# Four-layer GNN on one core: the attributes' copy issued behind the step gathers, first keys inside the histogram, equality matrices from bf16 rank numbers, half of the zero fills issued last by ScalarE

## The chip, the cores and the metric

The kernel runs on one core of a Trainium2 chip as one program. Its time is the device time in microseconds of one execution, given as the median of several. Engine names in rows: PE is TensorE (PEld its weight loads), DVE is VectorE, ACT is ScalarE, POOL is GpSimd, SP is SyncE, which here only issues DMAs. Sixteen DMA engines serve all queues of the core.

## The reference, cut to what matters

The input is a graph of 3125 nodes with 128 features, 50,000 edges sorted by destination (`src`, `dst`), and 64 attributes for each edge. Four layers follow one another, each on relu(layernorm(x)), each added to x:

```
L0 GCN:   h = (h * rsqrt(deg_out)) @ W; agg = segment_sum(h[src], dst) * rsqrt(deg_in) + b
          out = relu(layernorm(agg) * gamma + beta) + h
L1 attn:  q[dst] . (k[src] + e) / 4, e = edge_attr @ We; softmax over each dst; sum of (v[src] + e)
          8 heads of 16; skip, layernorm, gelu FFN, layernorm
L2 GAT:   two GAT layers (3 heads, then 1), softmax over each dst, elu between
L3 SAGE:  two mean aggregations with linear maps and batch norm
```

Out-degrees, in-degrees and, for the attention layers, which edges of a block share a destination, are computed on the device from `src` and `dst`.

## The kernel before, in words

Edges are padded to 50,176 (`EP`) and seen as 392 blocks of 128 (`CH`), and as 98 groups of 4 blocks (`NG`, `GC`). Each engine has its own program, written out by hand; semaphores order them, and each engine and each DMA queue goes through its list in order. The change touches the first part of the program, in three stages.

**Preparation.** SP lists `src` and `dst` in HBM (`esrc`, `edst`), then fills `eattr`, the attributes with each block of 128 rows turned round (`fill`, L690): that is a copy of 49,920 rows of 256 bytes. VectorE computes for 1172 "steps" (`STEPS`, in 10 chunks of 128, `NC`) which edge block and which quadruple of nodes each belongs to, and hands the indices to GpSimd, which gathers 128 rows of `esrc` and of `edst` for each chunk (L978, L981: 20 gathers, `step_edges`). Meanwhile VectorE builds one-hots of `src` for a histogram of out-degrees in 25 turns (`hot`, `HTURNS`; TensorE multiplies them, L1447), and then waits for all 20 gathers, turns those of the first two chunks (`SOON`) into keys (`key_steps`), and enters the loop. TensorE transposes the keys (`keys_of`), ScalarE copies them out (`keys_copied`).

**The adjacency loop**, 147 batches (`NB`) of 8 steps. For a batch VectorE writes two one-hots (`hot_steps`: 1024 and 800 elements a partition), TensorE multiplies them into counts (L1488), ScalarE copies these into the adjacency matrix of the chunk (L1080). VectorE is at most three batches ahead of TensorE. From batch 17 on TensorE also runs the GCN product of the chunk before (`spmm`, L1474). When a chunk is complete, SP stores its 3200 KB (`store_adj`, L740); two chunks' room is alternated. From batch 20 on (`SAME0`) VectorE makes in addition one equality matrix for each group, about three in four batches (`same`, L2136):

```
tt(same_b[:, r, :, :], dst_row[:, r, :, ::-1],
   bc(dst_i[:, g * GC:(g + 1) * GC]..., [P, GC, P]), ALU.is_equal)
```

It compares the destination of each edge of a block with those of all 128 edges of the block. `dst_row` holds a group's 512 destinations on every partition, loaded by SP as int32 four groups ahead (`load_dst_row`, L724, `UNROLL`), and `same_b` goes to HBM (`store_same`, L731). On SP's list each group is a store, a load, sometimes a zero fill of `starts_q` (L746, 28 fills of 896 KB with groups 10, 12, ... 64) and at eight groups an adjacency store.

**The node stage** behind the loop: TensorE ends the products and sums them by node; ScalarE and VectorE copy out (`pick`), in-degrees give the index lists, then linear maps, norms, and q, k, v. GpSimd scatters rows of q into `starts_q`, which must be zero by then (`s_zero`). The attention pass reads `eattr` by groups, transposes it on TensorE, and ScalarE copies it out (`attr_sb`).

Of the kernel before, what the change touches and what calls it, by code (L numbers as in the profile page):

```python
# [13 lines left out]
P = 128  # L14
# [55 lines left out]
LATE_AT = 5  # L70
SPANS_AT = 40
# [109 lines left out]
def gnn_stack_kernel(nc, out, x, src, dst, edge_attr_64, **w):  # L181
    ctx = ExitStack()
    with ctx:
# [3 lines left out]
        def sem(name):  # L187
            return ctx.enter_context(nc.semaphore(name))
# [9 lines left out]
        breaks = hbm("breaks", [CH + 1, P + 2])  # L198
        same_hbm = hbm("same_hbm", [NG, P, GC * P], BF16)
# [18 lines left out]
        dst_i = sb("dst_i", [P, CH], I32)  # L218
# [79 lines left out]
        def place(at, parts, *dims):  # L298
# [66 lines left out]
                             "dst_row": (P, (UNROLL, GC, P), I32)}, work_at)  # L365
        iota_two, lo_t, key_t, hot_e, hot_k, dst_row = (
            work[k] for k in ("iota_two", "lo_t", "key_t", "hot_e", "hot_k", "dst_row"))
        block_i = dst_row[:, 0, :, :].rearrange("p k e -> p (k e)")[:, 0:CH]
# [21 lines left out]
                        "lo_f": (P, (CH,), BF16), "hi_f": (P, (CH,), BF16)})  # L390
        src_r, dst_r, prev_r, src_rf, dst_rf, brk_r = (prep[k] for k in ("src_r", "dst_r", "prev_r", "src_rf", "dst_rf", "brk_r"))
        part_i, lo_f, hi_f = (prep[k] for k in ("part_i", "lo_f", "hi_f"))
# [10 lines left out]
            "rank_i": (P, (3, CH), I32), "pay": (P, (5, GC), I32), "attr_k": (P, (GC, ED), F32)})  # L403
# [21 lines left out]
        s_hist = sem("s_hist")  # L425
        wp = tuple(WEIGHTED)
# [12 lines left out]
        step_edges = sem("step_edges")  # L439
# [41 lines left out]
        FILLS = 16 * 4  # L481
        ZERO_PARTS = 28
# [107 lines left out]

        def units(ch):

            return slice(ch * DG, ch * DG + (DG if ch < NC - 1 else 1))
# [55 lines left out]
        def _(sp):  # L649
# [38 lines left out]
            def fill(o, i):  # L688
# [4 lines left out]
            fill(eattr[E - tail:E - tail + P - tail, :], zrow[0:P - tail, 0:ED])  # L693
            fill(eattr[EP - P:EP, :], zrow[:, 0:ED])
            fill(eattr[FULL * P + P - tail:FULL * P + P, :].rearrange("t (s c) -> s t c", s=2),
                 edge_attr_64[FULL * P:E, :].rearrange("t (s c) -> s t c", s=2)[:, ::-1, :])
            fill(eattr[0:FULL * P, :].rearrange("(t p) c -> t p c", p=P),
                 edge_attr_64[0:FULL * P, :].rearrange("(t p) c -> t p c", p=P)[:, ::-1, :])
# [21 lines left out]
            def load_dst_row(g):  # L720
                r = g % UNROLL
                if g >= UNROLL:
                    sp.wait_ge(same_done.sem, same_done.at("gcn", g, UNROLL))
                sp.dma_start(dst_row[:, r, :, :].rearrange("p k e -> p (k e)"),  # L724
                             edst[P + g * GC * P:P + (g + 1) * GC * P].rearrange("(a n) -> a n", a=1)
# [27 lines left out]
            for g in range(UNROLL):  # L753
                load_dst_row(g)
# [1896 lines left out]
```

## Time and profile before

| | us |
|---|---|
| median of 3 runs | 2823.56 |
| lowest, highest | 2819.49, 2824.34 |
| the profiled execution | 2818.55 |
| its span in the profile | 2816.9 |

| engine | busy us | share of the span |
|---|---|---|
| TensorE | 1962.1 | 70% |
| VectorE | 1420.3 | 50% |
| GpSimd | 1385.7 | 49% |
| ScalarE | 963.1 | 34% |

These shares are averages over stages with different limits. GpSimd's time, for instance, is spent on row gathers in the attention passes, which the change does not touch; a stage has to be looked at by itself. The rows below give busy time of each engine in four stretches that together are the first 458 us, and then single instructions. A value in brackets behind a row is how long the engine was idle before it, and what ended that.

### The profile page before, as it was taken

Reading aid. Unit: us, or ns where it says so; the run is one execution under the profiler, and the core shown is the slowest. Engines: PE = TensorE matmul, PEld = TensorE weight load, DVE = VectorE, ACT = ScalarE, POOL = GpSimd, SP = SyncE. Lnnn points to the kernel's source line nnn. Section 1 sums busy time; section 2 is a strip of 40 time slices with the busy share of each in tenths; the row PEclk is TensorE's granted clock in tenths of the full one; section 3 lists DMA queues with packets and bytes.
Section 4 is the critical chain, followed back from the end, with each engine's and each line's share of the span. In section 5 each row is a group of like instructions: output and inputs, shape, how many; then the busy total and the mean of one; then the engine's idle time right before and its main releaser. Section 6 shows DMA issues by size and latency. Waiting matters only on the chain.

```text
span 2816.9 us, 33483 instructions
## 1 busy us (share of the span) xinstructions
PE 1962.1 (70%) x10859; PEld 1352.9 (48%) x10859; DVE 1420.3 (50%) x3094; ACT 963.1 (34%) x2148; POOL 1385.7 (49%) x1417
## 2 busy tenths in 40 slices
PE   3477787488888885747777777744444445499998
PEld 2344455277777774523333334433333334266666
DVE  7778774477767775634544444422222223512414
ACT  4433323333333333834444443422222222301202
POOL 6000001777777773577777771567777774300000
PEclk9899898788998895868888886875555555799999
DMA  9499960499998982157777773325555553565461
GB/s 212 134 330 385 358 225 19 137 256 259 264 267 255 262 248 58 24 141 239 235 246 236 247 242 119 90 67 130 132 132 136 132 135 89 178 203 161 138 201 33
DMA packets 518583, 517.97 MB, mean 184 GB/s; under 512 B 153344, under 2 KB 463763, under 8 KB 517227
## 3 DMA queue, kind: packets, MB, share of 16 engines
q1 hardware_dynamic: 310349, 267.63, 31.1%
q0 software_dynamic: 50528, 115.22, 16.1%
q10 hardware_dynamic: 157534, 132.98, 15.3%
q8 instruction: 89, 1.46, 0.2%
q14 instruction: 83, 0.68, 0.1%
HBM read 301.53 MB, written 227.32 MB: 188 GB/s over the span
## 4 chain that ended last, share of the span: by engine, by line
POOL 40%; PE 21%; issue 16%; DVE 11%; DMA 8%; ACT 3%; SPq 1%; POOLq 0%; ACTq 0%; DVEq 0%
POOL arena L1049 36%; PE ps L1586 10%; DMA arena<-edst 4%; DVE arena L1994 3%; PE ps L1568 2%; POOL arena L981 1%; PE ps L1857 1%; DVE same_b L2136 1%; PE ps L1474 1%; PE ps L1679 1%; DMA arena<-t_gat,src_i 1%; PE ps L1705 1%; DVE arena L2458 1%; ACT arena L1080 1%; ACT arena L1290 1%
## 5 line engine op out<-in xcount | busy, mean ns | idle before, releaser
L1080 ACT ACTIVATE arena<-ps 128x774 f32<-128x774 f32 (+8 forms) x689 | 492.8, 729 | 1142.4 <-PE ps L1679 631.6
L1049 POOL DMA_INDIRECT arena<-t_gat,src_i x784 | 741.4, 946 | 238.9 <-issue 235.3
L1679 PE MATMUL ps<-arena 128*128 128x136 f32 (+2 forms) x2352 | 688.4, 454 | 86.6 <-DVE arena L2348 81.6
L1679 PEld LDWEIGHTS ps<-arena 128*128 128x128 f32 x2352 | 460.2, 259 | 238.9 <-DVE arena L2348 115.3
L1049 POOL DMA_INDIRECT arena<-t_attn,src_i x392 | 379.9, 969 | 127.8 <-issue 112.7
L2296 DVE TENSOR_TENSOR z_b<-arena 128x12 f32<-128x12 f32 (+1 forms) x196 | 33.7, 172 | 589.3 <-DMA arena<-t_gat,src_i 581.9
L1586 PE MATMUL ps<-arena 128*128 128x384 bf16 x1850 | 304.8, 328 | 35.2 <-DVE rec L2505 32.7
L1637 PE MATMUL ps<-ident,logit 128*64 128x128 f32 (+2 forms) x147 | 47.7, 324 | 384.8 <-DVE logit L2309 324.1
L1586 PEld LDWEIGHTS ps<-arena 128*128 128x128 bf16 x1850 | 181.6, 98 | 158.2 <-issue 40.5
L2348 DVE TENSOR_TENSOR arena<-arena,ps 128x1536 f32<-128x1536 f32 (+1 forms) x196 | 229.8, 1214 | 1.6 <-ACT arena L1219 1.6
L1637 PEld LDWEIGHTS ps<-ident,logit 128*64 128x64 f32 (+2 forms) x147 | 14.1, 96 | 429.7 <-DVE logit L2309 356.1
L1008 POOL TENSOR_TENSOR arena<-arena,r_L_gnn_gamma 128x512 f32<-128x512 f32 (+1 forms) x7 | 8.1, 1155 | 402.0 <-ACT arena L1290 401.9
L1994 DVE TENSOR_TENSOR arena<-arena 128x1024 bf16<-128x1024 bf16 (+1 forms) x344 | 204.8, 648 | 0.5 <-ACT arena L1080 0.5
L1474 PE MATMUL ps<-arena 128*128 128x385 bf16 x925 | 187.4, 345 | 0.0
L2288 DVE TENSOR_TENSOR arena<-arena,ps 128x1024 f32<-128x1024 f32 x98 | 119.2, 1216 | 130.1 <-DMA arena<-t_attn,src_i 100.6
L1080 ACT ACTIVATE arena<-same_b 128x512 f32<-128x512 bf16 x294 | 167.6, 621 | 28.0 <-DMA same_b<-same_hbm 28.0
L1080 ACT ACTIVATE arena<-arena 128x512 bf16<-128x512 f32 (+4 forms) x208 | 63.9, 307 | 274.5 <-DVE arena L2601 246.5
L1488 PE MATMUL ps<-arena 128*128 128x100 bf16 x1176 | 91.8, 226 | 86.4 <-DVE arena L1994 84.5
L2601 DVE TENSOR_REDUCE arena<-ps 128x128 f32<-128x384 f32 x74 | 36.2, 551 | 220.0 <-PE ps L1586 220.0
L1488 PEld LDWEIGHTS ps<-arena 128*128 128x128 bf16 x1176 | 73.4, 107 | 125.7 <-DVE arena L1994 113.4
L1619 PE MATMUL ps<-w_e,arena 64*128 64x128 f32 x784 | 123.8, 303 | 1.2 <-DVE arena L2288 1.2
L1629 PE MATMUL ps<-arena 128*128 128x128 f32 x784 | 121.8, 302 | 0.0
(319 smaller groups left out, 2595.3 us busy)
## 6 DMA issues: line engine op xcount, KB each, us to landing
ends_gat<-arena ACTq DMA_DIRECT2D x98, 774.0 KB, 6.7
arena<-adj_hbm SPq DMA_DIRECT2D x90, 640.0 KB, 4.6
same_b<-same_hbm SPq DMA_DIRECT2D x294, 128.0 KB
adj_hbm<-arena SPq DMA_DIRECT2D x9, 3200.0 KB, 13.1
ends_attn<-arena ACTq DMA_DIRECT2D x98, 272.0 KB, 5.3
ends_gat<-arena ACTq DMA_DIRECT2D x98, 258.0 KB, 5.0
arena<-edst SPq DMA_DIRECT2D x98, 256.0 KB, 5.9
starts_q<-zrow SPq DMA_DIRECT2D x28, 896.0 KB, 7.4
```

The source lines that it names most:

```text
L1049: g.indirect_dma_start(out=row_b[:, n % RB, k, 0:row_tab[p].shape[1]], out_offset=None, in_=row_tab[p], in_offset=bass.IndirectOffsetOnAxi ...
L1080: return a.activation(o, i, ACT.Copy)
L1474: i = mm(bank(4 + n % 4)[:, 0:3 * D + 1], lhs, xs0[:, t, 0:3 * D + 1], start=t == 0, stop=t == NT - 1)
L1488: i = mm(ps[:, at:at + KEYS], hot_e[:, b % 3, e // 2, :, e % 2], hot_k[:, b % 3, e // 2, :, e % 2], start=True, stop=True)
L1586: m = mm(bank(ch % 2 * 4 + dl)[:, 0:3 * D], ring[:, u % RING, at:at + P], xs1[:, t, :, :].rearrange("p s c -> p (s c)"), start=t == 0, sto ...
L1619: i = mm(bank((1, 6)[g % 2])[:, k * D:(k + 1) * D], at_t[:, g % 2, k * P:(k + 1) * P], w_e[:, :], start=True, stop=True)
L1629: i = mm(bank((3, 7)[g % 2])[:, k * D:(k + 1) * D], same_f[:, g % RB, k, :], q_b[:, g % UNROLL, k, :], start=True, stop=True)
L1637: nc.tensor.transpose(bank(TURN_BANK[p])[0:kh, 0:P], logit[:, i % 2, 0:kh], ident[:, :])\
L1679: i = mm(o, same_f[:, g % RB, k, :], msg[:, g % 4, k * W:(k + 1) * W], start=True, stop=True)
L1994: return tt(o, bc(iota_two[:, 0:parts, :].rearrange("p (a i) s -> p a i s", a=1), [P, n, parts, 2]), bc(values.rearrange("p (a i s) -> p a ...
L2288: tt(kv, kv, bc(bank((1, 6)[g % 2]).rearrange("p (k s c) -> p k s c", k=GC, s=1), [P, GC, 2, D]), ALU.add).then_inc(kve_done.sem, 1)
L2348: tt(m[:, :, 0:heads * nc_].rearrange("p k (h c) -> p k h c", h=heads), rows_v, e, ALU.mult).then_inc(msg_done.sem, 1)
```

## The change

1. **The attributes' copy.** SP waits for a new semaphore `attr_go`, which GpSimd raises behind its 20 gathers, before it copies the attributes; everything behind it on SP's list comes after it. The copy is now straight, without the turned blocks; ScalarE turns the columns when it copies the transposed attributes out. The gathers of the first two chunks have a semaphore of their own, those of the other eight another (`late_edges`).
2. **The keys of two chunks** are computed on VectorE behind turn 12 of the histogram (`KEYS_AT`), and transposed on TensorE there.
3. **Rank numbers.** VectorE numbers the distinct destinations within each block by four scans over the breaks between destinations. They are small integers, exact in bf16. ScalarE stores them (`erank`) and loads the first four groups' rows; SP loads the rest, 128 KB each in place of 256. The comparison is of bf16 with bf16, written in pairs like the one-hots.
4. **The zero fills.** SP issues 14 of 28, with groups 8, 12, ... 60; ScalarE issues the other 14 behind its last batch. GpSimd waits for all of them ahead of the first scatter, not ahead of the node stage.

```diff
@@ SP @@
+            fill(eattr[E:E + P, :], zrow[:, 0:ED])
+            fill(eattr[E + P:EP, :], zrow[0:EP - E - P, 0:ED])
+            sp.wait_ge(attr_go, 1)
+            fill(eattr[0:E, :].rearrange("(a n) c -> a (n c)", a=1000),
+                 edge_attr_64.rearrange("(a n) c -> a (n c)", a=1000))
...
-            for g in range(UNROLL):
-                load_dst_row(g)
...
-                if g >= 10 and g % 2 == 0 and g // 2 - 5 < ZERO_PARTS:
-                    zeros(starts["attn"], ZERO_PARTS, g // 2 - 5, 256)
+                if g >= 8 and g % 4 == 0 and g // 4 - 2 < ZERO_SOON:
+                    zeros(sp, starts["attn"], ZERO_PARTS, g // 4 - 2, 256)
@@ GpSimd @@
             for ch in range(NC):
+                landed = step_edges if ch < SOON else late_edges
...
+            pool.sem_inc(attr_go, 1)
             g.memset(xs0[:, :, 3 * D:XW], 1.0).then_inc(s_ones, 1)
...
-            pool.wait_ge(s_zero, ZEROS)
...
+                if j == 0:
+                    pool.wait_ge(s_zero, ZEROS)
                 scatter("attn", j)
@@ ScalarE @@
+            act.wait_ge(rank_done, 2)
+            act.dma_start(erank.rearrange("(a t e) -> t a e", a=QA, e=P), rank_b[:, :, :]).then_inc(rank_out, 16)
...
+            act.wait_ge(rank_out, 16)
+            act.wait_ge(step_cmp, 4)
+            for g in range(UNROLL):
+                act.dma_start(dst_row[:, g, :, :].rearrange("p k e -> p (k e)"), ranks_of(g)).then_inc(dst_row_in.of(g), 16)
             act.wait_ge(s_brk, BRKS)
             for b in range(NB):
...
+            for at in range(ZERO_SOON, ZERO_PARTS):
+                zeros(act, starts["attn"], ZERO_PARTS, at, 256)
             act.wait_ge(adj_out[0], 16 * (NC // 2))
...
-                    copy(at_t[:, g % 2, :], bank(0)[0:ED, :]).then_inc(attr_sb_done.sem, 1)
+                    copy(at_t[:, g % 2, :].rearrange("c (k e) -> c k e", k=GC),
+                         bank(0)[0:ED, :].rearrange("c (k e) -> c k e", k=GC)[:, :, ::-1]).then_inc(attr_sb_done.sem, 1)
@@ TensorE @@
+            pe.wait_ge(rank_done, 1)
+            for a in range(QA):
+                i = mm(bank(3)[:, a * CQ:(a + 1) * CQ], rank_r[:, a, :], ident[0:CQ, 0:CQ], start=True, stop=True)
+            i.then_inc(rank_ps, 1)
...
             for turn in range(HTURNS):
+                if turn == KEYS_AT + 1:
+                    pe.wait_ge(step_keys, 1)
+                    keys_of(0, SOON, 0, 1)
@@ VectorE @@
-            v.tensor_copy(dst_i[:, :], ps[:, BANK:BANK + CH]).then_inc(s_small, 1)
...
+            for a in range(QA):
+                i = v.tensor_tensor_scan(rank_r[:, a, ::-1], ones[0:CQ, :], brk_r[:, a, :], 0.0, ALU.mult, ALU.add)
+            i.then_inc(rank_done, 1)
+            dve.wait_ge(rank_done, 1)
+            v.tensor_copy(rank_b[:, :, :], rank_r[:, :, :]).then_inc(rank_done, 1)
...
             for turn in range(HTURNS):
                 hot(turn)
+                if turn == KEYS_AT:
+                    dve.wait_ge(step_edges, 16 * 2 * SOON)
+                    for part_of in key_steps(0, SOON, key_math, step_keys):
+                        part_of()
...
+            dve.wait_ge(rank_ps, 1)
+            v.tensor_copy(rank_two[:, :, :], bc(bank(3)[:, 0:CH].rearrange("p (c s) -> p c s", s=1), [P, CH, 2]))
             dve.wait_ge(s_hist, HTURNS)
...
-            dve.wait_ge(step_edges, 16 * 2 * NC)
-            for part_of in key_steps(0, SOON, key_math, step_keys):
-                part_of()
...
-                tt(same_b[:, r, :, :], dst_row[:, r, :, ::-1],
-                   bc(dst_i[:, g * GC:(g + 1) * GC].rearrange("p (k c) -> p k c", c=1), [P, GC, P]), ALU.is_equal)\
+                tt(same_b[:, r, :, :].rearrange("p k (i s) -> p k i s", s=2),
+                   dst_row[:, r, :, :].rearrange("p k (i s) -> p k i s", s=2),
+                   bc(rank_two[:, g * GC:(g + 1) * GC, :].rearrange("p k (i s) -> p k i s", i=1), [P, GC, P // 2, 2]),
+                   ALU.is_equal)\
```

On SP, at the end of the lists (`pad_i` holds the padding, `zrow` zeros, `edst` the destinations), before:

```order
L677 DMA edst<-pad_i 48x1
L690 DMA eattr<-zrow 48x64
L690 DMA eattr<-zrow 128x64
L690 DMA eattr<-in_edge_attr 2x80x32
L690 DMA eattr<-in_edge_attr 49920x1x64
L724 DMA arena<-edst 128x512 x4
```

and now, the third `eattr` row being the one that waits for GpSimd:

```order
L693 DMA edst<-pad_i 48x1
L706 DMA eattr<-zrow 128x64
L706 DMA eattr<-zrow 48x64
L706 DMA eattr<-in_edge_attr 256x12500
L669 DMA r_L_gnn_b<-in_L_gnn_b 128x128
```

The copy is cut into 256 long pieces in place of 49,920 short ones, and the four loads of the first groups' rows have left SP's list.

On VectorE in the middle of the histogram (the one-hots of 2048 and 400 elements are one turn), now:

```order
L2017 TENSOR_TENSOR arena<-arena 128x2048
L2017 TENSOR_TENSOR arena<-arena 128x400
L2037 TENSOR_SCALAR arena<-arena 128x256
L2038 TENSOR_SCALAR arena<-arena 128x256
L2042 CAST arena<-arena 128x256
L2043 TENSOR_SCALAR arena<-arena 128x256
L2047 TENSOR_TENSOR arena<-arena 128x256
L2048 TENSOR_SCALAR arena<-arena 128x256
L2052 TENSOR_TENSOR arena<-arena,step_f 128x256
L2057 SCALAR_TENSOR_TENSOR arena<-arena 128x256
L2017 TENSOR_TENSOR arena<-arena 128x2048
```

where before these eight stood behind the last turn:

```order
L1994 TENSOR_TENSOR arena<-arena 128x200
L2016 COPY deg<-ps 128x25
L2018 TENSOR_SCALAR norm<-deg 128x25
L2026 TENSOR_SCALAR arena<-arena 128x256
L2027 TENSOR_SCALAR arena<-arena 128x256
L2031 CAST arena<-arena 128x256
L2032 TENSOR_SCALAR arena<-arena 128x256
```

The eight key instructions are the same; twelve turns now come behind them.

On ScalarE behind the last batch copy (`arena<-ps 128x100x8` is a batch), now:

```order
L1185 ACTIVATE bn_a<-bn_a 128x256
L1087 ACTIVATE arena<-ps 128x100x8 x73
L603 DMA starts_q<-zrow 896x1x256 x14
L1087 ACTIVATE arena<-ps 128x391 x4
L1319 ACTIVATE norm<-norm 128x25
```

where before nothing stood between the 73 batch copies and the four copies of 391 elements.

## Rows read from the trace of the kernel before

**Rows 1.** Busy time by stretch: start:end, length, each engine's busy us, clock, DMA share.

```profile
0.00:86.45 86.45, 26.08 (x428) 19.72 (x428) 54.56 (x120) 31.11 (x133) 49.79 (x44) 1.00 0.93 215
86.45:130.20 43.75, 21.41 (x180) 16.22 (x181) 40.80 (x84) 27.95 (x53) 0.00 (x0) 0.73 0.21 52
130.20:400.80 270.60, 207.03 (x1812) 129.70 (x1811) 219.34 (x438) 105.19 (x128) 0.00 (x0) 0.90 0.93 335
400.80:458.00 57.20, 54.85 (x310) 39.12 (x309) 22.92 (x79) 5.09 (x7) 0.00 (x0) 0.94 0.25 93
```

**Rows 2.** Waits of VectorE in 86.45 to 400.8: total us, times, longest.

```profile
DVE same_b L2136 <- DMA arena<-edst: 51.0, 16, 7.9
DVE arena L2071 <- PE ps L1456: 2.9, 1, 2.9
```

**Rows 3.** Timeline of 0 to 105: start us, us, instruction, idle before.

```profile
26.39 52.21 SPq L724 DMA_DIRECT2D arena<-edst  x4
...
26.60 1.11 POOL L978 DMA_INDIRECT arena<-esrc,step_i  x1 [21.91 <-DMA edst<-pad_i]
...
28.02 26.79 POOL L981 DMA_INDIRECT arena<-edst,step_i  x1 [0.30 <-issue]
...
77.30 0.94 POOL L981 DMA_INDIRECT arena<-edst,step_i  x1 [0.30 <-issue]
...
82.20 0.30 DVE L2026 TENSOR_SCALAR arena<-arena 128x256 int32<-128x256 int32 x1 [18.95 <-DMA arena<-edst,step_i]
```

**Rows 4.** Groups by line and shape, 0 to 104: busy us, mean ns.

```profile
L1994 DVE TENSOR_TENSOR arena<-arena 128x2048 bf16<-128x2048 bf16 x24 | 29.3, 1220 | 0.0
...
L1994 DVE TENSOR_TENSOR arena<-arena 128x400 bf16<-128x400 bf16 x24 | 8.6, 360 | 0.0
```

**Rows 5.** The same of the attention pass, 550 to 1095.

```profile
L2319 DVE TENSOR_TENSOR_SCAN arena<-arena,ps 64x128 f32<-64x128 f32 x49 | 19.9, 405 | 6.9 <-PE ps L1637 6.9
```

**Rows 6.** The same of the adjacency loop, 104 to 455.

```profile
L1994 DVE TENSOR_TENSOR arena<-arena 128x800 bf16<-128x800 bf16 x140 | 79.5, 568 | 0.0
...
L2136 DVE TENSOR_TENSOR same_b<-arena,dst_i 128x512 bf16<-128x512 int32 x98 | 67.0, 684 | 51.2 <-DMA arena<-edst 51.0
```

**Rows 7.** DMA queue and issues, 160 to 340: KB each, us to landing.

```profile
q1 hardware_dynamic: 44133, 66.58, 101.7%
...
starts_q<-zrow SPq DMA_DIRECT2D x27, 896.0 KB, 7.4
adj_hbm<-arena SPq DMA_DIRECT2D x5, 3200.0 KB, 13.7
```

**Rows 8.** All DMA packets in 300 to 310, then in 310 to 320.

```profile
DMA packets 3324, 3.78 MB, mean 378 GB/s; under 512 B 161, under 2 KB 2806, under 8 KB 3323
...
DMA packets 877, 4.17 MB, mean 417 GB/s; under 512 B 75, under 2 KB 564, under 8 KB 748
```

**Rows 9.** Timeline around two adjacency stores of the loop.

```profile
250.69 0.69 DVE L2136 TENSOR_TENSOR same_b<-arena,dst_i 128x512 bf16<-128x512 int32 x1 [7.37 <-DMA arena<-edst]
...
372.26 0.49 SPq L740 DMA_DIRECT2D adj_hbm<-arena  x1
...
385.00 0.69 DVE L2136 TENSOR_TENSOR same_b<-arena,dst_i 128x512 bf16<-128x512 int32 x1 [3.62 <-DMA arena<-edst]
```

**Rows 10.** Timeline: an issue of ScalarE's, and its work behind the loop.

```profile
10.10 10.41 ACTq L1101 DMA_DIRECT2D x_sb<-in_x  x1
...
427.29 0.87 ACT L1080 ACTIVATE arena<-ps 128x391 f32<-128x391 f32 x1 [24.93 <-PE ps L1568]
...
449.03 0.22 ACT L1303 ACTIVATE norm<-norm 128x25 f32<-128x25 f32 x1 [12.31 <-DVE cnt_r L2210]
```

**Rows 11.** Chain of waits, 150 to 460: TensorE behind a wait, and later.

```profile
386.84 0.85 PE ps L1488 x8
387.69 1.93 PE ps L1474 x6
...
397.18 0.99 PE ps L1474 x6
398.17 0.38 PE ps L1488 x8
```

More of the change, by code:

```diff
@@ L70 @@
 LATE_AT = 5
+KEYS_AT = HTURNS // 2
 SPANS_AT = 40
@@ L198, in gnn_stack_kernel @@
         breaks = hbm("breaks", [CH + 1, P + 2])
+        erank = hbm("erank", [EP], BF16)
         same_hbm = hbm("same_hbm", [NG, P, GC * P], BF16)
@@ L364, in gnn_stack_kernel @@
                              "hot_e": (P, (3, BATCH // 2, P, 2), BF16), "hot_k": (P, (3, BATCH // 2, KEYS, 2), BF16),
[L365 to L368, printed above, removed]
+                             "block_i": (P, (CH,), I32), "dst_row": (P, (UNROLL, GC, P), BF16)}, work_at)
+        iota_two, lo_t, key_t, hot_e, hot_k, dst_row, block_i = (
+            work[k] for k in ("iota_two", "lo_t", "key_t", "hot_e", "hot_k", "dst_row", "block_i"))
         hist_at = work_at + P * BATCH // 2 + NC * P
@@ L959, in _ @@
                                                 (edst.rearrange("(e a) -> e a", a=1), 3, pay[:, 1, k:k + 1]),
-                                                (eattr, 4, attr_k[:, k, :])):
+                                                (eattr, 2, attr_k[:, k, :])):
                             g.indirect_dma_start(out=to, in_=what, in_offset=None, out_offset=bass.IndirectOffsetOnAxis(
@@ L1440, in _ @@
                 .then_inc(s_bnd, 1)
-            pe.wait_ge(step_cmp, 1)
-            for turn in range(HTURNS):
-                slot, n = turn % 2, min(WIDE, CH - turn * WIDE)
-                pe.wait_ge(s_hot, turn + 1)
-                for k in range(n):
-                    i = mm(bank(7)[:, 0:NT], hot_lo[:, slot, k // 2, :, k % 2], hot_hi[:, slot, k // 2, :, k % 2],
-                           start=turn == 0 and k == 0, stop=turn == HTURNS - 1 and k == n - 1, skip_group_check=True)
-                i.then_inc(s_hist, 1)
-            pe.wait_ge(step_keys, 1)
             def keys_of(c0, c1, lo_bank, key_bank):
@@ L1458, in keys_of @@
                     i.then_inc(keys_ps, 1)
-            keys_of(0, SOON, 0, 1)
+            pe.wait_ge(rank_done, 1)
+            for a in range(QA):
+                i = mm(bank(3)[:, a * CQ:(a + 1) * CQ], rank_r[:, a, :], ident[0:CQ, 0:CQ], start=True, stop=True)
+            i.then_inc(rank_ps, 1)
+            pe.wait_ge(step_cmp, 1)
+            for turn in range(HTURNS):
+                if turn == KEYS_AT + 1:
+                    pe.wait_ge(step_keys, 1)
+                    keys_of(0, SOON, 0, 1)
+                slot, n = turn % 2, min(WIDE, CH - turn * WIDE)
+                pe.wait_ge(s_hot, turn + 1)
+                for k in range(n):
+                    i = mm(bank(7)[:, 0:NT], hot_lo[:, slot, k // 2, :, k % 2], hot_hi[:, slot, k // 2, :, k % 2],
+                           start=turn == 0 and k == 0, stop=turn == HTURNS - 1 and k == n - 1, skip_group_check=True)
+                i.then_inc(s_hist, 1)
             def spmm(n, t0, t1):
```

92 lines of the change are left out of this document (45 added, 47 removed).

## The prediction

> **What bounds the kernel now.** I began with busy time by stretch [rows 1]. Everything that the change moves lies in the first three of four stretches: 86.5 us of preparation, 43.8 us for the first 20 batches of the adjacency loop, 270.6 us for the rest of the loop, 57.2 us for what follows it. Behind 458 us nothing is touched except the order in which `eattr` is read, so I keep that part as it is.
>
> In the third stretch VectorE is busy 219.3 us of 270.6. The waits of that engine [rows 2] hold 51.0 us in 16 pieces, all for the rows of `edst`, and 219.3 + 51.0 = 270.3: VectorE and its wait for one transfer fill the stretch. TensorE, busy 207.0 us, never keeps VectorE waiting there for more than 2.9 us.
>
> The preparation is read from the order of events [rows 3]. The attribute copy is the last thing SP issues ahead of 26.4 us; SP's next issue then takes 52.2 us, GpSimd's second gather 26.8 us instead of about 1. The 20 step gathers are out at 78.2 us. VectorE has ended its histogram at 63.3 and waits 18.95 us for them, computes the keys of two chunks until 84.8 and enters the loop at 86.45.
>
> **Preparation: -16 us.** With the copy held back, the second gather should cost 1.1 + 0.3 us like the others. The 18 gathers from 54.8 to 78.25 took 23.4 us, so the twenty run from 26.6 to about 53, and the four that the first keys need are out at 32, landed well under 40. A histogram turn is two one-hots, (29.3 + 8.6) / 24 = 1.58 us less the overlap of neighbours [rows 4], and 25 turns fill 27 to 63.3, that is 1.45 each. The keys come behind turn 12, at about 27 + 13 x 1.45 = 46: no wait. What the change adds on VectorE: four scans of 98x128 at 0.4 us (the nearest is a scan of the same length in the attention pass, 0.405 [rows 5]), one cast of about 0.4, the copy of rank pairs, 784 elements out of PSUM, at some 1.0 (the 512-element form takes 0.68), less a 0.5 us copy removed. So the histogram ends at 63.3 + 1.5 + 2.6 (the keys) = 67.4, and with rank pairs, reciprocal and two copies of 0.55 the loop begins at 70.4 instead of 86.45. Bounds: at most the wait of 18.95; at least 8, if TensorE's transposes or ScalarE's later relu hold things up. I take 16.
>
> **The equality matrices: -26 us.** 98 comparisons of 512 elements take 0.684 us each. The one-hots have the form that they get now, all bf16 with pairs innermost: 800 elements in 0.568, 400 in 0.360 [rows 4, 6], so 512 in 0.360 + 112 x 0.208/400 = 0.418. 98 x 0.266 = 26.1 us, in the stretch that VectorE fills, so on the path. Bounds: 0 if the form gains nothing, 34 if it halves. VectorE's work in the stretch becomes 193 us.
>
> **The wait for the rows: -8 us.** This is where I disagree with the plain reading. In 160 to 340 us SP's queue takes 101.7% of the 16 engines' time, with 27 fills of 896 KB and 5 adjacency stores of 3200 KB among the small ones [rows 7]. Slices of 10 us give the price of a packet: 3324 packets with 3.78 MB against 877 with 4.17 MB [rows 8], both full. Solved for a + b x bytes that is about 7 ns a packet and 37 ns a KB on one engine: 2.5 us of all engines for a fill, 7.9 for an adjacency store, 0.66 for a row load of 256 KB and 0.36 for one of 128 KB. The loop's transfers shrink by 14 x 2.5 + 98 x 0.3 = 64 us and are no longer its bound.
>
> But the wait is not spread over the queue. Each of the eight adjacency stores in the loop is followed by one long wait. The store issued at 372.26, with no fill near it, is followed by a row load that lands at 385.00 and a wait of 3.62 us; a wait among the fills, ended at 250.69, was 7.37 us [rows 9]. Rows are loaded four groups ahead, 8.9 us of VectorE's pace (219.3 / 98 a group), and that load landed 12.7 us after the store was issued. The change leaves store and order alone. It makes four groups 1.1 us shorter (4 x 0.266) and the load about 0.5 us quicker: a store without a fill costs 3.6 + 1.1 - 0.5 = 4.2 us, one with a fill just ahead (groups 36, 48, 60) 2.0 more, the one behind the GAT fills 5.8, the first 5. Sum 5 + 2 x 4.6 + 3 x 6.3 + 5.8 + 4.2 = 43 against 51: 8 us. Bounds: 15 left if the backlog of fills was what made each wait long, 60 if VectorE's faster pace counts for more.
>
> **The fills that ScalarE issues last: +2 us.** Fourteen fills are 35 us of all engines, issued from 402 on, beside the last 4 MB of adjacency. ScalarE's next work is four PSUM copies, the first at 427.3, and a square root at 449.03 that VectorE waits for [rows 10]; 449.0 less 4 x 0.87 leaves it until 445.5, 43 us after its last batch copy. GpSimd wants the fills only at its first scatter, later in the node stage. What can hurt is that a queue takes only so much: ScalarE's issue behind the 1.5 MB load of x took 10.41 us [rows 10]. If two fills fit, it is held for 12 x 2.5 + 10 = 40 us: just short. Bounds 0 and +60. In the Trainium skill, page DMA: Bandwidth & Descriptors, section Issuing engines are not separate DMA queues, the time to initiate a DMA is "usually small relative to the DMA itself"; by it ScalarE would be free after 14 issues of about 0.5 us (an adjacency store's took 0.49), 7 us, and this term would be nothing. The row of 10.41 us speaks against it. The same page, section Queues, rings and completion order, has each engine alternate between queues packet by packet; no row of before shows two full queues of this kind. By that the last adjacency store would land near 421 instead of 412, still ahead of the 424 at which VectorE asks for it.
>
> **Sum.** The profiled execution took 2818.55 us (span 2816.9). 2818.55 - 16 - 26 - 8 + 2 = 2770.5. It lies 5 us under the median of the runs, 2823.56; set against that, 2775.5. I predict 2775.
>
> **Rivals.**
> The fills make the waits (0.17). For it: the waits with fills near are about twice those without [rows 9]. Against it: 3.62 and more remain where there is none. With 15 us left instead of 43, 2747.
>
> TensorE becomes the bound (0.15). At a granted clock of 1.0 a batch's one-hots take it 0.38 us and six of its 6.25 products 0.99; right behind a wait, at half the clock, 0.85 and 1.93 or more [rows 11]. A full-speed batch is 1.41 us, VectorE's would be 1.52 (193 us over 127 batches). Per adjacency chunk TensorE needs 16 x 1.41 = 22.6 and 4.5 more where some 9 us run at 1.2 GHz: 27.1, against 24.3 plus the wait on VectorE. If it cannot use the wait to catch up, 8 x 2.5 = 20 us are lost: 2795. Against it: VectorE never waited for it, and three batches of buffer cover most of this.
>
> The bf16 comparison is no faster (0.05): 2801.
>
> The copy is late (0.07). It now heads SP's queue at 53, with all weights and row loads behind; it must be through by about 113, when the first comparison is due, which asks 213 GB/s. The old one moved the same bytes in 52 us beside other work [rows 3], which is 246. At 150 GB/s it costs 25 us: 2800.
>
> ScalarE is held by its fills, and the kernel is slower (0.04). If its queue takes one fill at a time, each costs its 7.4 us to land [rows 7]: 14 x 7.4 = 104 us, free at 506 instead of 445.5, and the node stage starts 60 us late: 2835. It costs nothing until ScalarE is held 43 us, and eats the whole gain at 93.
>
> **How the numbers follow.** The forecast has 0.52, with 2760 to 2790 as its own range. 0.2% of the time (5.6 us) is about what a measurement can tell from no change. All cases but the last are faster by more: 0.94 faster, 0.02 same, 0.04 slower. The range 2745 to 2800 takes in the other faster cases and leaves out the slow one and the far ends.
>
> **What would show it.** Right: step gathers out by 55 us, no wait of VectorE for them, loop begun at 69 to 72; the comparisons at 0.42 us; waits for `erank` rows of 4 to 6 us, one behind each adjacency store, 43 us together; VectorE at 193 us in the loop's second part, which ends near 350; ScalarE's fourteen issues taking some 40 us and its square root following at once. Wrong: waits spread or gone, TensorE's batches waited for by VectorE, or the scatters of q waiting for fills.

## The result

The changed kernel takes 2803.01 us (median of 4 runs, 2800.59 to 2806.59) where the kernel before takes 2823.31 on the same chip: a ratio of 0.9924, 95% interval 0.9903 to 0.9946. The profiled execution's span is 2799.0 us, against 2816.9. It is faster, as forecast, but by 20 us and not by 48; 2775 was predicted and the range ended at 2800.

### The profile page after: what moved, and what is told of

It reads as the page before. It is cut to its first block, busy times and chain, and to the rows that moved or that the text cites. A ratio compares the mean times of both kernels' runs of the same rounds, so it can differ in the third digit from the quotient of the medians.

```text
span 2799.0 us, 33506 instructions
## 1 busy us (share of the span) xinstructions
PE 1968.7 (70%) x10867; PEld 1366.0 (49%) x10867; DVE 1393.9 (50%) x3099; ACT 964.0 (34%) x2148; POOL 1381.6 (49%) x1417
## 4 chain that ended last, share of the span: by engine, by line
POOL 38%; PE 23%; issue 16%; DVE 12%; DMA 8%; ACT 2%; SPq 0%; POOLq 0%; ACTq 0%; DVEq 0%
POOL arena L1056 34%; PE ps L1607 10%; DVE arena L2017 3%; DMA arena<-erank 3%; PE ps L1589 2%; PE ps L1700 2%; PE ps L1878 1%; DMA arena<-t_attn,src_i 1%; PE ps L1495 1%; DMA arena<-edst,step_i 1%; POOL arena L983 1%; DVE same_b L2163 1%; DMA ends_gat<-arena 1%; PE ps L1726 1%; DVE arena L2487 1%
```

## The profile after

Busy time by stretch, in the columns of [rows 1]. The stretches are cut where VectorE ends the histogram, begins the loop's second batch and ends the loop, and where ScalarE first multiplies by the norm in the node stage (called the first norm below).

```profile
0.00:70.52 70.52, 27.88 (x429) 21.39 (x430) 54.45 (x118) 29.16 (x128) 42.08 (x43) 0.68 0.45 124
70.52:102.18 31.66, 1.22 (x16) 0.92 (x16) 4.67 (x12) 2.81 (x7) 1.10 (x2) 0.50 0.96 297
102.18:379.94 277.76, 217.40 (x1993) 146.89 (x1994) 231.11 (x519) 133.02 (x181) 0.00 (x0) 0.87 0.72 246
379.94:436.55 56.61, 54.34 (x303) 39.20 (x302) 23.02 (x79) 3.87 (x7) 0.00 (x0) 0.94 0.90 312
```

The third stretch, of the kernel before:

```profile
88.75:401.68 312.93, 228.49 (x1993) 145.96 (x1994) 257.88 (x520) 133.81 (x182) 0.00 (x0) 0.87 0.83 296
```

The second row of after is the surprise: a stretch of 31.66 us in which VectorE does 4.67 us of work and the DMA engines are 96% busy. The third says that the rest of the loop did what was forecast: it is 35.2 us shorter, with 26.8 us less work on VectorE.

VectorE's waits from 60 to 400 us, as in [rows 2]:

```profile
DVE same_b L2163 <- DMA arena<-erank: 40.9, 10, 6.7
DVE arena L2037 <- DMA arena<-edst,step_i: 26.1, 1, 26.1
DVE vdeg L2172 <- PE ps L1495: 6.4, 2, 3.5
DVE arena L2098 <- PE ps L1462: 3.5, 1, 3.5
```

The timeline of the preparation, beside [rows 3]:

```profile
27.96 1.03 POOL L986 DMA_INDIRECT arena<-edst,step_i  x1 [0.31 <-issue]
29.30 18.75 POOL L983 DMA_INDIRECT arena<-esrc,step_i  x1 [0.30 <-issue]
48.36 0.94 POOL L986 DMA_INDIRECT arena<-edst,step_i  x1 [0.30 <-issue]
...
50.85 0.33 DVE L2037 TENSOR_SCALAR arena<-arena 128x256 int32<-128x256 int32 x1 [3.62 <-DMA arena<-edst,step_i]
...
54.57 0.51 SPq L706 DMA_DIRECT2D eattr<-in_edge_attr  x1
...
70.52 0.94 POOL L986 DMA_INDIRECT arena<-edst,step_i  x1 [0.31 <-issue]
...
73.71 1.16 DVE L2017 TENSOR_TENSOR arena<-arena 128x1024 bf16<-128x1024 bf16 x2
...
100.97 0.69 DVE L2037 TENSOR_SCALAR arena<-arena 128x1024 int32<-128x1024 int32 x1 [26.10 <-DMA arena<-edst,step_i]
```

Three things are to be seen. With no attribute copy running, one gather of GpSimd's still takes 18.75 us. SP issues the copy at 54.57, when 8 of the 20 gathers have begun: the semaphore that the code puts behind them does not wait for them. And the last gather, issued at 70.52, lets VectorE go on only at 100.97. The loop begins at 73.71, 12.7 us earlier than before, stops after its first batch, and has its second batch at 102.18, 13.4 us later than before (88.75).

The issues from 24 to 130 us (KB each, median us to landing) name what the gathers met:

```profile
q1 hardware_dynamic: 6416, 15.53, 47.6%
...
eattr<-in_edge_attr SPq DMA_DIRECT2D x1, 12500.0 KB, 44.3
arena<-erank ACTq DMA_DIRECT2D x4, 128.0 KB, 28.9
...
arena<-esrc,step_i POOLq DMA_INDIRECT x10, 19.2
```

Written as a few long rows, the copy's 12.5 MB go in packets of some 50 KB, as the same view of 60 to 70 us alone shows (63 packets for 3.15 MB on q1):

```profile
q1 hardware_dynamic: 63, 3.15, 92.1%
q0 software_dynamic: 65, 0.14, 7.8%
...
arena<-edst,step_i POOLq DMA_INDIRECT x4, 30.7
arena<-esrc,step_i POOLq DMA_INDIRECT x4, 30.9
```

Queue q1 carries the copy, q0 the gathers: 65 small packets for 63 large ones. Before, where the copy went by blocks of 256-byte rows, the last gather was issued at 77.30 and VectorE went on at 82.20 [rows 3].

ScalarE behind the loop, beside [rows 10]:

```profile
379.79 43.40 ACTq L603 DMA_DIRECT2D starts_q<-zrow  x14
423.29 2.96 ACT L1087 ACTIVATE arena<-ps 128x391 f32<-128x391 f32 x4 [42.67 <-issue]
427.26 0.23 ACT L1319 ACTIVATE norm<-norm 128x25 f32<-128x25 f32 x1 [1.01 <-DVE cnt_r L2239]
```

The fourteen issues hold it 43.4 us, and its square root still waits for VectorE alone. From the end of the loop to the first multiplication by the norm it is 56.6 us, and was 56.7 before.

## The experiments

The times are medians. The kernel before was measured again beside each batch of runs and stood at 2820.4 to 2823.3 us; "gain" is how far a kernel's median lies below that of the kernel before beside it. The 95% interval of a kernel that ran four times is 6 to 8 us to either side, so a difference of a few us between two kernels is not read from the times alone. "Second batch" and "loop end" are read from each profile as above (102.18 and 379.94 in the changed kernel). The gathers begin at different times in different profiles (at 26.4 us in the changed kernel, at 31.8 with the rank numbers in F32), so the length between the two columns is safer than either.

| kernel | us | gain | second batch | loop end | waits for rows |
|---|---|---|---|---|---|
| before | 2823.3 |  | 88.75 | 401.7 | 51.0 |
| changed | 2803.0 | 20.3 | 102.18 | 379.9 | 40.9 |
| copy behind landed gathers | 2796.5 | 23.9 | 76.71 | 371.7 | 58.8 |
| copy in 1.28 KB pieces | 2779.3 | 41.1 | 78.37 | 355.7 | 42.6 |
| copy in 6.4 KB pieces (one run) | 2780.1 | 42.1 | 81.19 | 360.8 | 43.2 |
| copy early, 1.28 KB pieces | 2790.0 | 33.2 | 84.33 | 364.4 | 44.4 |
| copy late, and a gap on VectorE | 2780.9 | 39.5 | 73.11 | 359.3 | 51.2 |
| kernel before with that gap alone | 2805.1 | 18.1 | 74.97 | 386.8 | 50.8 |
| rank numbers in F32 | 2823.2 | -0.9 | 108.79 | 409.4 | 39.8 |
| all fills by SP | 2815.4 | 6.8 | 102.28 | 392.5 | 52.2 |
| adjacency stores in quarters | 2786.6 | 33.8 | 105.74 | 365.4 | 23.2 |
| four edits together | 2759.5 | 63.7 | 72.66 | 333.5 | 24.5 |
| the same, all fills by SP | 2784.3 | 38.8 | 77.68 | 362.3 | 46.2 |
| four edits, quarters spread | 2741.0 | 81.3 | 73.09 | 321.8 | 12.7 |

### What made the gathers late

**The copy behind the landed gathers.** GpSimd's sequencer waits for the data, not only for its own place in the list:

```diff
+            pool.wait_ge(late_edges, 16 * 2 * (NC - SOON))
             pool.sem_inc(attr_go, 1)
```

> The changed kernel, but SP issues the attribute copy only when all ten step gathers have landed (GpSimd's sequencer waits for the semaphores of the late gathers before it passes SP on). Theory (the late gathers of the changed kernel landed only at about 101 us because SP's copy had begun at 54.6 us, before they were issued): VectorE's longest wait of the preparation, 26.1 us at the loop's first key arithmetic, falls to 5 to 8 us (the gathers go out until about 71 us and land some 4 us later), the copy is issued at 73 to 78 us, and the median falls from 2803 to about 2783 us (2778 to 2788). Rival (the gathers are late by themselves, whatever runs beside them): the wait stays near 26 us and the median at 2800 to 2806. Second rival (the copy moved into the loop takes its time from the rows there): the wait is gone, but the waits for rows of 41 us grow by as much, and the median stays at 2795 or above.

The copy is now issued at 75.51 us, and the wait of 26.1 us is one of 1.17:

```profile
75.46 0.70 DVE L2038 TENSOR_SCALAR arena<-arena 128x1024 int32<-128x1024 int32 x1 [1.17 <-DMA arena<-edst,step_i]
```

So the cause of the lateness is as the theory says. The time is not: by the gains 3.6 us were won, by the medians 6.5, and neither is clear of the noise, because the second rival holds as well. The waits for rows grow from 40.9 to 58.8 us. The two longest:

```profile
140.97 0.43 DVE L2164 TENSOR_TENSOR same_b<-arena,rank_two 128x512 bf16<-128x512 bf16 x1 [14.89 <-DMA arena<-erank]
149.31 0.43 DVE L2164 TENSOR_TENSOR same_b<-arena,rank_two 128x512 bf16<-128x512 bf16 x1 [6.82 <-DMA arena<-erank]
```

and SP's list behind the copy:

```profile
75.51 0.51 SPq L706 DMA_DIRECT2D eattr<-in_edge_attr  x1
...
81.32 27.07 SPq L669 DMA_DIRECT2D r_L_gnn_b<-in_L_gnn_b  x1
...
136.81 0.43 SPq L739 DMA_DIRECT2D arena<-erank  x1
```

Some 30 small weight loads stand behind the copy on SP's list. The issue of one of them takes 27 us, SP is through with them at 136, and only then comes the next row load, which VectorE had wanted since 126.

**Small pieces at the same place.**

```diff
-            fill(eattr[0:E, :].rearrange("(a n) c -> a (n c)", a=1000),
-                 edge_attr_64.rearrange("(a n) c -> a (n c)", a=1000))
+            fill(eattr[0:E, :].rearrange("(a b r) c -> a b (r c)", a=16, b=625)[:, ::-1, :],
+                 edge_attr_64.rearrange("(a b r) c -> a b (r c)", a=16, b=625)[:, ::-1, :])
```

> The changed kernel, with the attribute copy issued at the same place and time and of the same bytes, but in 10,000 pieces of 1.28 KB (16 rows of 625 pieces, in reversed order so that they stay apart) instead of 50 KB packets. Theory (what held the gathers was the size of the copy's packets, behind each of which a gather's small packet waits its turn): the gathers land within 4 to 8 us of their issue beside the copy, where it was 31 us, VectorE's wait of 26.1 us falls below 8, and the median comes to 2778 to 2788 us. Rival (what counts is only that the copy's 25.6 MB of reads and writes were issued ahead of them): the gathers still take 25 to 31 us, and the median stays at 2798 to 2806.

The expectation is met: 2779.3 us, 21 less than the changed kernel by the gains and 24 by the medians. VectorE's row is

```profile
77.16 0.70 DVE L2037 TENSOR_SCALAR arena<-arena 128x1024 int32<-128x1024 int32 x1 [2.49 <-DMA arena<-edst,step_i]
```

The copy is issued at 54.37, as early as in the changed kernel, and takes as long to land (45.8 us against 44.3). Bytes, time and order of issue are the same; only the packets differ. The prediction spent a rival on when the copy would be through and none on what its packets would be.

**6.4 KB pieces**, the same with `b=125`.

> The changed kernel with the attribute copy at its place in 2,000 pieces of 6.4 KB, between the 1.28 KB pieces already tried and the 50 KB packets of the changed kernel. Theory (the time that a gather's packets wait grows with the size of the packets they take turns with): the last gather lands 8 to 16 us after its issue, where it was some 29 us behind 50 KB packets and 6 behind 1.28 KB, and the run takes 2780 to 2792 us. Rival (any piece small enough to be apart is as good): it lands within 6 us, as with 1.28 KB.

```profile
79.98 0.70 DVE L2037 TENSOR_SCALAR arena<-arena 128x1024 int32<-128x1024 int32 x1 [5.29 <-DMA arena<-edst,step_i]
```

From the last gather's issue to VectorE's next step it is 8.4 us (71.59 to 79.98). With 1.28 KB it is 6.8 (70.32 to 77.16), with 50 KB 30.5 (70.52 to 100.97), and 4.3 with no copy beside it (71.20 to 75.46). The time grows with the packets, but not in proportion: by 1.6 us from 1.28 to 6.4 KB, by 22 us from there to 50 KB. Each of the four is read from one profile, and the time of 2780.1 us is that of one run. The Trainium skill, page DMA: Bandwidth & Descriptors, section Queues, rings and completion order, says that an engine serves its queues in turn and changes only between packets; these four numbers agree with it. The prediction drew on that section for the last adjacency store, and did not apply it to the copy.

**The copy where it was, in 1.28 KB pieces:** the wait for `attr_go` goes.

> The changed kernel without the wait ahead of the attribute copy: SP issues it at about 20 us, as in the kernel before, but in pieces of 1.28 KB. Theory (to move the copy behind the gathers bought nothing, since it never held them; late and in 50 KB packets it cost 26 us): the preparation ends as in the kernel with small pieces, the loop starts near 71 to 75 us with 3 to 8 us of waiting, and the median is 2776 to 2786 us. Rival (the copy beside the first gathers does slow them): the loop starts 10 us or more later and the median is 2790 or above.

The theory falls, narrowly: the median is 2790.0 us, and the second batch at 84.33 is 6 us later than with the late copy in the same pieces (the rival said 10). The first keys pay for it:

```profile
57.99 0.30 DVE L2036 TENSOR_SCALAR arena<-arena 128x256 int32<-128x256 int32 x1 [10.72 <-DMA arena<-edst,step_i]
```

where that wait is 3.6 us with the copy behind them. So the copy does slow the landing of gathers that it runs beside. What its later issue is worth is less sure: 4 us at the second batch, since this profile's gathers also began 2.2 us later; 8 us by the gains and 11 by the medians, with intervals that overlap (0.9867 to 0.9911 against 0.9834 to 0.9882).

### What held GpSimd

**A gap on VectorE.** In both kernels one gather lasts until VectorE, which had written one-hots without a pause, leaves off for the first time. After, the gather ends at 48.05, and VectorE stands still from 47.23. Before, it ends at 54.81, and from 53.89 to 54.42 VectorE does two operations of 25 elements between its one-hots:

```profile
53.89 0.30 DVE L2011 RECIPROCAL rs<-sd 128x25 f32<-128x25 f32 x1
54.23 0.19 DVE L2013 TENSOR_TENSOR nm<-nm,rs 128x25 f32<-128x25 f32 x1
```

So the long gather might not be the copy's doing at all.

```diff
                 hot(turn)
+                if turn == 1:
+                    dve.wait_ge(s_hist, turn + 1)
```

> As the kernel whose copy waits for the landed gathers, and in addition VectorE stands still once at the histogram's turn 1, until TensorE has done that turn. Theory (GpSimd's third gather lasted 18.75 us, until VectorE's first gap at 47 us, because VectorE had worked without a gap on two-input bf16 operations): with a gap at about 31 us the third gather ends at 31 to 34 us, the later ones follow at 1.4 us each and are out at 55 to 58 us, VectorE's waits of 3.6 us (first keys) and of 5 to 8 us (late gathers) are both gone, and the median is 6 to 10 us below that of the late copy alone. Rival (the gather is held by its own work, or by a DMA resource): it still ends near 48 us and the median is within 3 us of the late copy alone.

The gap (0.74 us) and GpSimd's gathers around it:

```profile
29.48 3.22 POOL L983 DMA_INDIRECT arena<-esrc,step_i  x1 [0.30 <-issue]
...
32.62 8.29 DVE L2018 TENSOR_TENSOR arena<-arena 128x2048 bf16<-128x2048 bf16 x11 [0.74 <-PE ps L1480]
33.00 1.66 POOL L986 DMA_INDIRECT arena<-edst,step_i  x1 [0.30 <-issue]
...
55.88 1.11 POOL L986 DMA_INDIRECT arena<-edst,step_i  x1 [0.30 <-issue]
```

The gather takes 3.22 us instead of 18.75, the last one is issued 15 us earlier, and both waits for gathers are gone. The median is 15.6 us below that of the late copy alone, more than the 6 to 10 expected. The copy and the weights behind it are earlier too (59.74 instead of 75.51), and with them the first rows: the wait of 14.89 us is 6.64.

**The same line in the kernel before, and nothing else.**

> The kernel before with one wait added and nothing else: at the histogram's turn 1 VectorE waits until TensorE has done that turn. Theory (in the kernel before, too, the second gather's 26.8 us were VectorE's unbroken run of two-input bf16 operations, not the attribute copy that ran beside it): that gather ends at 30 to 35 us, the later ones are out by about 60, VectorE's wait of 18.95 us for the keys' gathers is gone, and the median falls from 2820 to 2799 to 2805 us, as much as the whole change brought. Rival (the attribute copy's DMA traffic held the gathers, as the prediction had it): the gather still lasts over 20 us, the wait stays over 15 us, and the median is 2816 to 2824.

```profile
32.51 2.83 POOL L981 DMA_INDIRECT arena<-edst,step_i  x1 [0.31 <-issue]
...
35.23 6.88 DVE L1994 TENSOR_TENSOR arena<-arena 128x2048 bf16<-128x2048 bf16 x9 [0.72 <-PE ps L1447]
...
60.19 1.55 POOL L981 DMA_INDIRECT arena<-edst,step_i  x1 [0.30 <-issue]
...
72.67 1.18 DVE L1994 TENSOR_TENSOR arena<-arena 128x1024 bf16<-128x1024 bf16 x2 [0.46 <-ACT arena L1080]
```

The median is 2805.1 us, a ratio of 0.9936 (0.9915 to 0.9956): within the noise, one wait of 0.72 us gives what the whole change gave (0.9924). The loop from its second batch is as long as before, 311.8 us against 312.9. The gather ends at 35.34 and the last one goes out at 60.19, although this profile's gathers began 4.4 us later, and the attribute copy runs beside them as before. That the 26.8 us of [rows 3] were the copy's is refuted. The Trainium skill, page SBUF — State Buffer, section Who interferes with whom, has VectorE and GpSimd share a pair of SBUF ports as an exclusive lock; that fits the gap, but not that one gather stays locked out over more than a dozen VectorE instructions while the later ones, beside the same instructions, go on at 1.4 us each (56.67, 58.08, 59.49 in the kernel before). Why only the first long stretch blocks is open. So is what the gap alone would give in the changed kernel, with its copy as it is: that was not run.

### The loop's terms

**The rank numbers in F32:** the rows, the tile compared with, and the array in HBM. To make room, `block_i` now lies in the first rows' place.

```diff
-        rank_two = sb("rank_two", [P, CH, 2], BF16)
+        rank_two = sb("rank_two", [P, CH, 2], F32)
-                             "block_i": (P, (CH,), I32), "dst_row": (P, (UNROLL, GC, P), BF16)}, work_at)
+                             "dst_row": (P, (UNROLL, GC, P), F32)}, work_at)
...
+        block_i = dst_row[:, 0, :, :].rearrange("p k e -> p (k e)").bitcast(I32)[:, 0:CH]
...
```

> The changed kernel with the rank numbers in F32 instead of BF16: the rows that are loaded, the tile they are compared with and the array behind them; the comparisons stay where they are. Theory (the step of the prediction on the comparisons was right): one comparison takes 0.68 us instead of 0.42, which is 26 us for 98; the rows' loads are twice as large, as in the kernel before, and add 0 to 10 us of waiting; the loop from its second batch on takes 305 to 315 us instead of 277.6, and the median is 2828 to 2840 us. Rival (the comparisons are hidden beside TensorE): the median is within 8 us of 2803.

The comparisons in the changed kernel, and in this one (shortest, median and longest in ns):

```profile
L2163 DVE TENSOR_TENSOR same_b<-arena,rank_two x98: 357/416/426, 144.2 to 377.8; 128x512 bf16<-128x512 bf16 x98
L2164 DVE TENSOR_TENSOR same_b<-arena,rank_two x98: 631/686/701, 150.5 to 408.5; 128x512 bf16<-128x512 f32 x98
```

A comparison takes 0.686 us against 0.416, and from the second batch to the loop end it is 300.6 us against 277.8: 22.8 of the 26.5 us that the comparisons add are on the path. The theory's direction holds, but it asked for more: 305 to 315 us there and a median of 2828 to 2840, where 2823.2 was measured, 20.2 above the changed kernel (21.2 by the gains). The rows' waits are 39.8 us, against 40.9. That does not say that their size of 256 KB costs nothing, since the slower comparisons also give each load more time (4 x 0.27 us for four groups); the two together come to 1.1 us.

**All 28 fills by SP**, one behind every second group.

```diff
-        ZERO_PARTS, ZERO_SOON = 28, 14
+        ZERO_PARTS, ZERO_SOON = 28, 28
-                if g >= 8 and g % 4 == 0 and g // 4 - 2 < ZERO_SOON:
-                    zeros(sp, starts["attn"], ZERO_PARTS, g // 4 - 2, 256)
+                if g >= 10 and g % 2 == 0 and g // 2 - 5 < ZERO_SOON:
+                    zeros(sp, starts["attn"], ZERO_PARTS, g // 2 - 5, 256)
```

> The changed kernel with all 28 zero fills issued by SP again, one behind every second group, and none by ScalarE behind the loop. Theory (fourteen fills fewer in the loop were worth 10 to 25 us, as they were in the kernel with all four edits, and more than the 8 us of the prediction; ScalarE's issuing behind the loop is hidden): the waits for rows rise from 41 to 52 to 62 us and the median to 2812 to 2826 us. Rival (a fill costs only where quarters of stores stand before it; here the ten stalls are those of the whole adjacency stores either way): waits of 41 to 49 us and a median of 2798 to 2810.

```profile
DVE same_b L2163 <- DMA arena<-erank: 52.2, 15, 8.3
```

The waits are 52.2 us instead of 40.9 and the median is 12.4 us higher: the theory is met, and the fills that ScalarE took over were worth 12 us net.

**Adjacency stores in quarters.** Each is issued as four, behind four successive groups.

```diff
-                sp.dma_start(o, i).then_inc(adj_out[ch % 2], 16)
+                n = (KEYS * P if ch < NC - 1 else KEYS * LAST) // ADJ_Q
+                sp.dma_start(o[:, q * n:(q + 1) * n], i[:, q * n:(q + 1) * n]).then_inc(adj_out[ch % 2], 16)
...
+                at = [(ch, q) for ch in range(NC - 1) for q in range(ADJ_Q) if groups_by((ch + 1) * PER + 3) + ADJ_EVERY * q == g]
```

> The changed kernel with each adjacency store issued as four quarters, one behind each of four successive groups' row loads, instead of whole. Theory (the ten stalls, 40.9 us in all, come from row loads that stand behind a whole store of 13.7 us on the DMA queues, while VectorE has but four groups of rows ahead): a quarter of 3.4 us stands before each load, and the stalls fall from 40.9 to below 15 us; the loop ends 25 to 35 us earlier and the median is 2768 to 2780 us. Rival (the DMA queues, busy at over 0.8 in the loop, lack bandwidth, whatever the order): the stalls are only spread over more groups and stay at 35 us or more, and the median is 2798 to 2806 us.

```profile
DVE same_b L2167 <- DMA arena<-erank: 23.2, 22, 2.4
```

The result lies between the two: the waits fall from 40.9 to 23.2 us, in 22 pieces instead of 10, the longest 2.4. The loop from its second batch takes 259.7 us against 277.8, 18.1 less where 25 to 35 were expected. The median falls by 16.4 us (13.5 by the gains). The granted clock of TensorE from 160 to 360 us is 0.98 to 1.00. In the changed kernel, where TensorE stands idle in VectorE's stalls, it was 0.91 to 0.93.

### Together

The four edits: the gap, the copy behind the landed gathers in 1.28 KB pieces, the weight loads ahead of it on SP's list, and the quarters.

```diff
...
                 for o, i in weights:
                     load(o, i)
+            sp.wait_ge(attr_go, 1)
+            fill(eattr[0:E, :].rearrange("(a b r) c -> a b (r c)", a=16, b=625)[:, ::-1, :],
+                 edge_attr_64.rearrange("(a b r) c -> a b (r c)", a=16, b=625)[:, ::-1, :])
```

> The changed kernel with all that the runs so far point to: VectorE's gap at the histogram's turn 1; the attribute copy behind the landed gathers, in pieces of 1.28 KB, and issued behind the small weight loads instead of ahead of them; each adjacency store as four quarters behind four groups. Theory (the gains are of separate causes and add up, since the loop starts at 71 us and its rows wait 23 us instead of 41 to 51): the loop ends at 335 to 342 us, the median is 2755 to 2765 us. Rival (with the loop shorter, ScalarE's fourteen fills, 44 us of issuing behind the loop, or TensorE in the loop give part of it back): the loop ends there but the median is 2768 or above.

The median is 2759.5 us, a ratio of 0.9777 (0.9762 to 0.9793), as the theory had it. Of the 43.5 us under the changed kernel, the late copy and the gap gave 22.1 when they were run together, and the quarters 16.4; the other 5 fall to the small pieces and the weights' place, which were not run apart here. The small pieces gave 24 alone, but they and the landed gathers remove the same wait of 26.1 us, so those two do not add up. The loop ends at 333.5, and ScalarE's fills still hide: from loop end to the first norm it is 56.6 us again.

**The same with all 28 fills by SP.**

> As the kernel with all four edits, but with all 28 zero fills issued by SP, one behind every second group, as in the kernel before, and none by ScalarE. Theory (the fills compete with the rows: fourteen more fills of 7.4 us among 98 groups raise the DMA share of the loop to about 1): the waits for rows rise by 10 to 25 us and the loop ends as much later, but ScalarE's 44 us of issuing behind the loop are gone; the median is 5 to 15 us above that of the kernel with all four edits. Rival (the fills cost nothing where they stand between quarters of stores, and ScalarE's issuing is what holds the node stage): the median is equal or lower by up to 15 us.

The median is 2784.3 us, 24.8 more, where 5 to 15 were expected, and the waits are 46.2 us instead of 24.5. The loop from its second batch takes 284.6 us against 260.8, 23.8 more. The rival that the fills are free between quarters is refuted.

**The quarters behind every second group** (`ADJ_EVERY = 2`).

> As the kernel with all four edits, but the quarters of an adjacency store stand behind every second group instead of behind four successive ones. Theory (the 24.5 us of waiting for rows that were left come where quarters and zero fills stand behind the same groups and the queue gets more than a group's time of traffic each time): spread over eight groups, the waits fall to 8 to 16 us and the median to 2744 to 2755 us. Rival (what is left is the DMA queues' bandwidth, whose share is already 0.94 in mid loop, or the next store comes too near the next chunk's first copies): no gain, 2756 or above.

```profile
DVE same_b L2170 <- DMA arena<-erank: 12.7, 15, 1.7
```

The median is 2741.0 us, a ratio of 0.9713 (0.9700 to 0.9727) to the kernel before: the fastest here, at a DMA share of 0.95 from 160 to 260 us. It beat its own expectation by 3 us. The rival held that bandwidth was the limit; at a share of 0.94 with 24.5 us of waits against 0.95 with 12.7, the order on the list decided. From loop end to the first norm it is 58.3 us here, where it was 56.6. That is not ScalarE's fills: it is 58.2 in the kernel before with the gap alone too, where ScalarE issues no fill, and in these two profiles a run of 50 small multiplications behind the loop takes TensorE 8.3 and 8.5 us, against 6.3 to 7.4 in the profiles with 56.6.

## Why the prediction was wrong

**The step that failed is the preparation, -16 us.** Counted from VectorE's second batch it was +13.4. The loop did begin 12.7 us earlier (73.71 against 86.45), and later than the 70.4 forecast mainly by the 3.6 us of waiting at the first keys, and the added operations cost what was put down (the rank pairs 0.97 us, said 1.0). But it stood still for 26.1 us after its first batch. Three things in that step were wrong:

1. "With the copy held back, the second gather should cost 1.1 + 0.3 us". It was VectorE's unbroken work that held it. With no copy running, another gather took 18.75 us in the changed kernel; with the copy running, the second gather of the kernel before took 2.83 us once VectorE paused. The gathers were out at 71.5 and not at 53; that alone cost the 3.6 us at the first keys.
2. The copy was taken to start behind the gathers. It started at 54.57, when twelve of them had yet to begin: here the semaphore raised behind the gathers on GpSimd's list did not wait for them. Made to wait for their data, it started at 75.51.
3. The copy's new shape was read as bandwidth only. In 50 KB packets it held for 30 us gathers that land in 4 without it, which cost VectorE 26.1 us. In 1.28 KB packets issued at the same time it cost 2.5. This is the largest of the three.

The rival "the copy is late" (0.07) had its time nearly right, 2800, for another reason: it feared for the rows at 113 us, which the copy did not touch in the changed kernel. That fear came true in the kernel whose copy is later still.

**The other terms held.** The comparisons: -26 said; 26.8 us less work on VectorE at 0.416 us each (0.418 said), and 20 to 23 us when undone. The waits for rows: 43 said, one behind each of the eight adjacency stores, and 40.9 in 10 pieces measured. That the order of the stores makes most of them, with the same bytes to move, is shown by the quarters. The make-up of this term held too: its sum has VectorE's faster pace and the quicker loads at 8 x (1.1 - 0.5), about +5 us, and so the missing fills at about -13; measured, pace and size together are worth 1.1 us and the fills 11.3. ScalarE's fills: 40 us held said, 43.4 measured; +2 said, nothing to be seen. The margin was as thin as the prediction said: it put the limit at 43 us, and ScalarE then waited 1.0 us for VectorE. Second batch to loop end, -26 - 8 = -34 said, -35.2 measured.

**The sum.** +13.4 - 35.2 = -21.8 us at the loop's end (401.68 to 379.94); -21.8 at the first norm (458.39 to 436.55); -17.9 over the span. About 4 us of the gain are lost again behind the first norm; over all kernels the time from the first norm to the end runs from 2357 to 2366 us with no pattern that the edits explain, so they are not assigned. With the preparation at -16 in place of +13.4, 2803 becomes 2774, against the 2775 that was forecast. That the two larger of the other terms held is no luck, as shown above; that it fits to 1 us is, since no term stood for the 4 us lost behind the first norm.

**Of the rivals**, "the fills make the waits" was part true: the fourteen fills make 11.3 us in the changed kernel and 21.7 with quarters, but 40.9 stayed without them and not 15. "TensorE becomes the bound" is refuted: with the waits at 12.7 us the loop takes 248.7 us from its second batch, 29 less than in the changed kernel, and TensorE keeps up at a granted clock of 0.96. "The bf16 comparison is no faster" is refuted by the 0.416 us. "ScalarE held, and slower" did not happen.

## What to carry to other kernels

When a transfer is reshaped, write down the size of its packets as well as its bytes, and what small transfers other queues will have under way beside it. Before an engine's long instruction is put down to the DMA traffic next to it, look at what the other engines did in the same microseconds, and above all at the instant when it ended. A signal that stands behind transfers on an engine's list need not come behind the transfers; where it must mean "the data is there", wait for the data's own semaphore. And where a wait recurs behind one large transfer, try cutting that transfer up along the list before looking for bandwidth: here that took the waits from 40.9 to 23.2 us, and with wider spacing from 24.5 to 12.7, with as many bytes moved.

## What the runs showed of the hardware

- Small gathers beside a 12.5 MB copy took 30.5 us to be usable at 50 KB packets, 8.4 at 6.4 KB, 6.8 at 1.28 KB, and 4.3 without it (one profile each).
- A GpSimd gather stayed under way 18.75 to 26.8 us while VectorE wrote bf16 one-hots back to back, and 2.8 to 3.2 us when VectorE paused for 0.7 us early on. The later ones ran beside the same work at 1.4 us each.
- A semaphore raised on GpSimd's list behind 20 gathers arrived 17 us before the last of them was done (54.57 against 71.46).
- An issue can hold its engine far longer than its own 0.5 us: 18 to 38 us for a 64 KB load behind the copy, 43 to 45 for fourteen fills.
